# Copying the second key stack on GpSimd, and placing the scores ahead of the second turned half

## The chip, the cores and the metric

One core of a Trainium2 chip runs the whole kernel in one launch. The metric is the device time in microseconds; the median of three runs of the kernel before is 1804.26 us (1802.96 to 1804.39).

## What is computed

A transformer layer on x of 4 batches, 1024 tokens, 256 features, in float32: a layer norm, DeBERTa-style attention with 16 heads of 16 features, a residual, then a layer norm and a feed-forward with 8 experts, picked per token, and a residual again. The change lies in the attention:

```python
scores = einsum('bhqd,bhkd->bhqk', q, k) / scale
c2p = take_along_axis(einsum('bhqd,hpd->bhqp', q, pos_k), c2p_pos, -1)     # by distance, 128 buckets
p2c = swapaxes(take_along_axis(einsum('bhkd,hpd->bhkp', k, pos_k), p2c_pos, -1), -1, -2)
probs = softmax(scores + (c2p + p2c) / scale)
ctx = einsum('bhqk,bhkd->bhqd', probs, v)
```

The bucket depends on the distance q - k alone, and beyond 128 tokens it is constant on either side. So only the three 128x128 blocks around the diagonal need the gathered values (the kernel calls them near), and for all others two constants per row do.

## The kernel before

The program has four stages: `project` (up to about 135 us of the profiled execution), `attend` (to about 1350 us), `mix` and `experts`. The change is in `attend` (L570). There are N = 64 units, one for each batch and head, and each has QT = 8 steps, one for each block of 128 queries; s counts steps over all units, t is the step in a unit, x counts tables. Every engine runs its own loop over s and waits on semaphores, so its order is what the Python text says.

**TensorE** (loop at L822) does in step s, in this order: the first half of a turned block, `flip(back, 0)`, for the block back = s - 13; the position table of block x = s + 20 (`make_table`, two matmuls at L743 and L745 into the one bank `table_ps`); the second turned half `flip(back, 1)`; the scores `score(s)` of block s; in every second step `weigh` for two blocks (sums of probabilities times values, L810); and once per unit, at t = 1, `turn_top` (L818). A flip makes 512 columns of transposed scores in one of two PSUM banks `flip_ps` (L789 for far blocks, L796 for near ones). It waits for `expd`, the exponential that read the same bank one block earlier. `make_table` waits for `table_kept` of the table before, and at t = 2 also for `top_kept`, since the turned row maxima use the same bank. `score(s)` (far blocks L766, near blocks L773) waits for `seen` of block s - 2, at t = 0 for `twin_made` and the loads, and ahead of L773 for `near_made`. With j for the block of `back` within its unit, j = (t + 3) mod 8.

**ScalarE** (loop at L954) does in step s: `exponent(back, 0)` (L932), `keep_table` (L924 and L925, the table from PSUM into `table`), `exponent(back, 1)`; at t = 4 the `twin` of the next unit (L938: the key stack `after`, 96 partitions x 1024 bfloat16, is copied into `before`, the second key stack, whose other rows differ); at the end of a unit's flips `keep_sum`; and at t = 1 `keep_top`: a copy (L944) and a DMA issue (L946) that puts the row maxima into `quest`, where `flip` of j = 0 needs them (`top_in`, L782).

**VectorE** (L906) does in step s `look(s)`: the maximum of the far scores (L849), then `level(s - 1)` (L870), then near scores plus near table with the row maximum (L859, this signals `seen`); and once per unit `normalise` (L878 to L885; L882 is its multiplication).

**GpSimd** (L1040) makes the near part of a unit out of what DMAs bring: five steps `edge` (L995, L998, L1003, L1008, L1011) for each of two parts h = 0 (three blocks) and h = 1 (five blocks), placed by the list `steps` (L1033); each part ends in one count of `near_made`. It also does `keep_side` (L983) and, at t = 7, `split_top` (L1021 to L1031), which waits for `seen` of the whole unit and feeds `turn_top`.

**SP** (L703) is a queue of DMA issues, in order, with waits between them. For each u: `skew_write(u+2, 0)` puts half of a unit's tables into DRAM with a pitch that skews them, `skew_read(u+1, 1)` reads the skewed near part h = 1 back, `load_unit(u+4)` loads queries and keys (four DMAs, L178; it waits until the flips of the unit that used the buffers are done), every second time `load_far`, `skew_write(u+2, 1)`, `skew_read(u+2, 0)`, `store(u-3)`. A `skew_read` waits for the landing of its `skew_write` (L690). Ahead of the loop stands `load_unit(2)`.

Of the kernel before, what the change touches and what calls it, by code (L numbers as in the profile page):

```python
# [21 lines left out]
N = B * H  # L22
QT = S // P
# [18 lines left out]
KROWS = TERMS * DH  # L42
# [5 lines left out]
BUFS = 6  # L48
HATS = 4
# [520 lines left out]
def attend(nc, sem, spent, masks, rows, hats, split_d, far_d, v_d, skew_d, ctx_d):  # L570
# [13 lines left out]
    with ExitStack() as ctx:  # L584
# [43 lines left out]
        def live(s):  # L628

            return 0 <= s < TS  # L630
# [31 lines left out]
        def _(sp):  # L662
# [36 lines left out]
                sp.dma_start(view(ctx_d, n * (P * 2 * P), [[2 * P, P], [1, 2 * P]]), made[n % 2][:, :]  # L699
                             ).then_inc(ctx_out[n % 2], 16)  # L700

            load_unit(EARLY)
            for u in range(-2, N + 3):  # L703
                if 0 <= u + 2 < N:
                    skew_write(u + 2, 0)
                if 0 <= u + 1 < N:
                    skew_read(u + 1, 1)
                if EARLY < u + 4 < N:
                    load_unit(u + 4)
                if EARLY <= u + 2 < N and u % FARS == 0:  # L710
                    load_far(u + 2)
                if 0 <= u + 2 < N:
                    skew_write(u + 2, 1)
                    skew_read(u + 2, 0)
                if 0 <= u - 3 < N:
                    store(u - 3)
                if u == 1:
                    for semaphore in spent:
                        sp.sem_clear(semaphore)
                if u % BATCH == 4 and u // BATCH + 1 < B:  # L720
                    load_vals(u // BATCH + 1)
# [4 lines left out]
        def _(pe):  # L726
# [95 lines left out]
            for s in range(-AHEAD, TS + LAG + 1):  # L822
                back = s - LAG
                if live(back):
                    flip(back, 0)
                if live(s + AHEAD):
                    make_table(s + AHEAD)
                if live(back):
                    flip(back, 1)
                if live(s):  # L830
                    score(s)
                if live(back - 1) and back % 2 == 0:
                    weigh(back - 2)
                    weigh(back - 1)
                if s > QT and s % QT == 1 and s // QT <= N:
                    turn_top(s // QT - 1)
# [78 lines left out]
        def _(act):  # L915
# [16 lines left out]
                nc.scalar.activation(probsT[s % 4][:, half * 512:(half + 1) * 512], flip_ps[half][:, :], ACT.Exp,  # L932
                                     scale=SCALE).then_inc(expd, 1)

            def twin(n):
                i = n % BUFS
                act.wait_ge(hats_in[i], 16 * HATS * (n // BUFS + 1))
                nc.scalar.copy(before[i][0:KROWS, :], after[i][0:KROWS, :]).then_inc(twin_made, 1)  # L938

            def keep_top(n):  # L940
                act.wait_ge(top_turned, n + 1)
                if n >= 2:
# [11 lines left out]
            for s in range(-AHEAD, TS + LAG + 1):  # L954
                if s == 6 - AHEAD:
                    act.wait_ge(set_up, 4)
                    act.wait_ge(before_set, 3)
                    for dst, src in ((quests[KROWS:FAR, :, :], ones[0:3, :]), (afters[FAR:ROWS, :, :], after_rows[:, :]),
                                     (befores[FAR:ROWS, :, :], before_rows[:, :])):
                        nc.scalar.dma_start(dst, src.unsqueeze(1).to_broadcast([dst.shape[0], BUFS, S])).then_inc(rows_set, 16)  # L960
                if s == 10 - AHEAD:
                    hats.load_vals(nc.scalar, v_d, 0)
                back = s - LAG
                if live(back):
# [2 lines left out]
                    keep_table(s + AHEAD)  # L967
                if live(back):
                    exponent(back, 1)
                if s % QT == 4 and 0 <= s // QT + 1 < N:  # L970
                    twin(s // QT + 1)
                if live(back - 1) and (back - 1) % QT == QT - 1:
                    keep_sum((back - 1) // QT)
                if s > QT and s % QT == 1 and s // QT <= N:
# [3 lines left out]
        def _(pool):  # L978
            def keep_side(n, h):
                wait_tables(pool, n * QT + 4 * h + 3)  # L980
                if n >= 3:
                    pool.wait_ge(edge_made, (n - 3) * 10 + 10)
                nc.gpsimd.tensor_copy(side[n % 3][:, :, 4 * h:4 * h + 4], table[n % 2][:, h, :, :, BAND]).then_inc(side_kept, 1)  # L983

            def edge(n, h, step):
                i = n % 2
# [53 lines left out]
            for s in range(-AHEAD, TS):  # L1040
# [5 lines left out]
                for at, h, of in steps:  # L1046
                    n = (s - at) // QT + 1
                    if (s - at) % QT == 0 and 0 <= n < N:
                        for step in of:
                            edge(n, h, step)  # L1050
                if live(s) and t == QT - 1:
                    split_top(u)

# [697 lines left out]
```

## Time and profile before

| | us |
|---|---|
| median of three runs | 1804.26 |
| the profiled execution, its time | 1804.36 |
| its span in the profile | 1802.5 |
| PE busy in the span | 1630.6 (90%) |
| DVE busy | 1350.3 (75%) |
| ACT busy | 1135.2 (63%) |
| POOL busy | 1035.2 (57%) |

PE is TensorE, PEld its weight loads, DVE VectorE, ACT ScalarE, POOL GpSimd, SP the queue of SyncE. The spans of matmuls overlap, since they are pipelined, and their ends are modelled; the distance from start to start tells more than the durations. The busy shares are means over four stages; the middle of the attention, where unit follows unit in the same pattern, is what the rows below show.

### The profile page before, as it was taken

Reading aid. Unit: us, or ns where it says so; the run is one execution under the profiler, and the core shown is the slowest. Engines: PE = TensorE matmul, PEld = TensorE weight load, DVE = VectorE, ACT = ScalarE, POOL = GpSimd, SP = SyncE. Lnnn points to the kernel's source line nnn. Section 1 sums busy time; section 2 is a strip of 40 time slices with the busy share of each in tenths; the row PEclk is TensorE's granted clock in tenths of the full one; section 3 lists DMA queues with packets and bytes.
Section 4 is the critical chain, followed back from the end, with each engine's and each line's share of the span. In section 5 each row is a group of like instructions: output and inputs, shape, how many; then the busy total and the mean of one; then the engine's idle time right before and its main releaser. Section 6 shows DMA issues by size and latency. Waiting matters only on the chain. (4 is left out here: it accounts for less than half of the span.)

```text
span 1802.5 us, 41947 instructions
## 1 busy us (share of the span) xinstructions
PE 1630.6 (90%) x13688; PEld 1149.4 (64%) x13688; DVE 1350.3 (75%) x3868; ACT 1135.2 (63%) x2764; POOL 1035.2 (57%) x1264
## 2 busy tenths in 40 slices
PE   7964899999999999999999999999986856999997
PEld 4532566666666666666666666666643646999996
DVE  4754888888888888888888888888956854555553
ACT  6852677777777777777777777777753731222221
POOL 0004776777777777777777777777714622333332
PEclk9985999999999999999999999999996957999998
DMA  4977888788787878788878787777608625666661
GB/s 138 331 279 249 265 284 261 257 265 273 261 282 262 282 253 276 243 278 275 274 252 272 258 277 252 264 266 263 229 13 206 207 71 183 204 191 197 206 197 63
DMA packets 292451, 421.67 MB, mean 234 GB/s; under 512 B 35382, under 2 KB 233804, under 8 KB 292139
## 3 DMA queue, kind: packets, MB, share of 16 engines
q1 hardware_dynamic: 271640, 378.99, 64.3%
q10 hardware_dynamic: 16851, 30.67, 5.5%
q0 software_dynamic: 3744, 9.31, 1.4%
q8 instruction: 112, 1.84, 0.4%
q14 instruction: 104, 0.85, 0.1%
HBM read 241.39 MB, written 177.79 MB: 233 GB/s over the span
## 5 line engine op out<-in xcount | busy, mean ns | idle before, releaser
L932 ACT ACTIVATE t_probsT<-t_flip 128x512 f32<-128x512 f32 x1024 | 612.8, 623 | 204.2 <-PE t_flip L796 122.3
L849 DVE TENSOR_REDUCE t_most<-t_scores 128x1 f32<-128x640 f32 (+1 forms) x512 | 436.1, 852 | 157.8 <-PE t_scores L773 157.2
L859 DVE CUSTOM_DVE_ANT_0 t_band<-t_scores,t_near,t_most 128x384 f32<-128x384 f32 (+1 forms) x512 | 297.3, 581 | 0.5 <-DVE t_most L849 0.2
L870 DVE TENSOR_SCALAR_CACHE_REDUCE t_band<-t_band,t_top 128x384 f32<-128x384 f32 (+1 forms) x512 | 291.2, 569 | 0.0
L924 ACT COPY t_table<-t_table_ps 128x388 f32<-128x388 f32 x502 | 248.5, 495 | 48.1 <-PE t_table_ps L745 45.0
L810 PE MATMUL t_sum_ps<-t_probsT,vals 128*32 128x256 f32 x4096 | 274.3, 385 | 0.3 <-ACT t_probsT L932 0.3
L1011 POOL TENSOR_TENSOR t_near<-t_near,masks 128x768 f32<-128x768 f32 (+1 forms) x128 | 268.4, 2097 | 0.0
L796 PE MATMUL t_flip<-masks,t_band 128*128 128x128 f32 x1408 | 260.0, 273 | 0.0
L773 PE MATMUL t_scores<-masks,t_near 128*128 128x128 f32 x1408 | 241.9, 275 | 14.8 <-POOLq L1014 14.7
L766 PE MATMUL t_scores<-afters,quests 105*128 105x256 bf16 (+3 forms) x1024 | 244.0, 288 | 1.2 <-DVE t_top L859 1.2
L995 POOL TENSOR_TENSOR t_near<-t_near,masks 128x384 f32<-128x384 f32 (+1 forms) x128 | 146.2, 1142 | 168.6 <-DMA t_near<-skew_d 164.3
L773 PEld LDWEIGHTS t_scores<-masks,t_near 128*128 128x128 f32 x1408 | 181.8, 143 | 54.0 <-POOLq L1014 16.6
L766 PE MATMUL t_scores<-befores,quests 105*128 105x256 bf16 (+3 forms) x768 | 193.2, 292 | 0.0
L789 PE MATMUL t_flip<-quests,afters 108*128 108x512 bf16 (+3 forms) x512 | 159.4, 311 | 11.9 <-ACT t_probsT L932 10.2
L789 PE MATMUL t_flip<-quests,befores 108*128 108x512 bf16 (+3 forms) x512 | 159.2, 313 | 9.1 <-ACT t_probsT L932 4.1
L796 PEld LDWEIGHTS t_flip<-masks,t_band 128*128 128x128 f32 x1408 | 163.0, 141 | 3.3
L743 PE MATMUL t_table_ps<-rows,quests 96*128 96x194 bf16 x502 | 126.6, 252 | 42.4 <-ACT t_table L925 18.2
L810 PEld LDWEIGHTS t_sum_ps<-t_probsT,vals 128*32 128x32 f32 x4096 | 106.8, 109 | 87.4 <-issue 41.2
L1717 PEld LDWEIGHTS e_hid_ps<-e_xT,e_w 128*128 128x128 f32 x1248 | 147.3, 194 | 5.2 <-ACT e_xT L1583 3.2
L1717 PE MATMUL e_hid_ps<-e_xT,e_w 128*128 128x128 f32 x1248 | 147.9, 277 | 2.6 <-ACT e_xT L1583 2.6
L925 ACT COPY t_table<-t_table_ps 128x124 f32<-128x124 f32 x502 | 146.7, 292 | 0.0
L1008 POOL TENSOR_TENSOR t_near<-t_near,masks 128x384 f32<-128x384 f32 (+1 forms) x128 | 146.4, 1144 | 0.0
(212 smaller groups left out, 2546.2 us busy)
## 6 DMA issues: line engine op xcount, KB each, us to landing
skew_d<-t_table SPq DMA_DIRECT2D x128, 1024.0 KB, 9.6
t_near<-skew_d SPq DMA_DIRECT2D x128, 640.0 KB, 8.0
t_near<-skew_d SPq DMA_DIRECT2D x128, 384.0 KB, 7.5
e_w<-in_L_ffn_W_dram ACTq DMA_DIRECT2D x39, 512.0 KB
e_w<-in_L_ffn_W_dram SPq DMA_DIRECT2D x39, 512.0 KB
split_d<-p_part SPq DMA_DIRECT2D x32, 384.0 KB, 3.3
afters<-split_d SPq DMA_DIRECT2D x128, 96.0 KB
quests<-split_d SPq DMA_DIRECT2D x128, 96.0 KB
```

What stands on the lines that cost most here:

```text
L766: nc.tensor.matmul(out[:, at:at + size], quest[i][0:XROWS, t * P:(t + 1) * P], keys[0:XROWS, piece[0] * P:piece[0] * P + size], start=at % ...
L773: last = nc.tensor.matmul(out[:, (j - lo) * P:(j - lo + 1) * P], near[n % 2][:, 1, j, (t - j + 1) * P:(t - j + 2) * P], ident, start=False ...
L789: last = nc.tensor.matmul(out[:, (a - lo) * P:(z - lo) * P], keys[:, j * P:(j + 1) * P], quest[i][:, a * P:z * P], start=first, stop=False ...
L796: last = nc.tensor.matmul(out[:, (t - lo) * P:(t - lo + 1) * P], band[n % 2][:, t, at:at + P], ident, start=False, stop=True, is_transpose ...
L810: last = nc.tensor.matmul(sum_ps[32 * g:32 * g + 32, 0:2 * P], vals[b % 2][:, j, h * VDIM:h * VDIM + 32], probsT[s % 4][:, g * 2 * P:(g + ...
L849: nc.vector.tensor_reduce(most[:, c:c + 1], out[:, wide:S], AX.X, ALU.max).then_inc(far_seen, 1)
L859: nc.vector.tensor_tensor_reduce(band[n % 2][:, t, 0:wide], out[:, 0:wide], near[n % 2][:, 0, t, at:at + wide], 1.0, most[:, c:c + 1], ALU ...
L870: nc.vector.tensor_scalar(band[n % 2][:, t, 0:wide], band[n % 2][:, t, 0:wide], top[n % 2][:, t:t + 1], None, ALU.subtract, ALU.max, accum ...
L924: nc.scalar.copy(ends, table_ps[:, :, 0:FEW].rearrange("p a (e v) -> p a e v", e=2))
L932: nc.scalar.activation(probsT[s % 4][:, half * 512:(half + 1) * 512], flip_ps[half][:, :], ACT.Exp, scale=SCALE).then_inc(expd, 1)
L1011: nc.gpsimd.tensor_tensor(tail, tail, masks[:, 1, :].unsqueeze(1).unsqueeze(1).to_broadcast([P, 2, many, P]), ALU.mult).then_inc(edge_made, 1)
L1717: last = nc.tensor.matmul(hid_ps[s % 2][:, c, :], w1[s % WB][:, f, c * P:(c + 1) * P], xT[s % 2][:, f, :], start=(f == 0), stop=(f == 1))
```

## The change

- GpSimd makes the second key stack: `twin` moves from ScalarE's loop (t = 4) to GpSimd's (t = 2, after the `edge` step of that slot).
- On TensorE `score(s)` stands ahead of `flip(back, 1)`; before it stood behind it.
- On the SP queue `load_unit(2)` and `skew_read(0, 0)` swap sides: the read of the first near part comes right behind `skew_write(0, 0)`, and `load_unit(2)` behind the read. Only then comes `skew_write(0, 1)`.
- ScalarE issues the first load of the values at s = 0 and no longer at s = -10.

```diff
--- before.py
+++ after.py
@@ -699,18 +699,20 @@
                 sp.dma_start(view(ctx_d, n * (P * 2 * P), [[2 * P, P], [1, 2 * P]]), made[n % 2][:, :]
                              ).then_inc(ctx_out[n % 2], 16)
 
-            load_unit(EARLY)
             for u in range(-2, N + 3):
                 if 0 <= u + 2 < N:
                     skew_write(u + 2, 0)
                 if 0 <= u + 1 < N:
                     skew_read(u + 1, 1)
-                if EARLY < u + 4 < N:
+                if u == -2:
+                    skew_read(0, 0)
+                if EARLY <= u + 4 < N:
                     load_unit(u + 4)
                 if EARLY <= u + 2 < N and u % FARS == 0:
                     load_far(u + 2)
                 if 0 <= u + 2 < N:
                     skew_write(u + 2, 1)
+                if 1 <= u + 2 < N:
                     skew_read(u + 2, 0)
                 if 0 <= u - 3 < N:
                     store(u - 3)
@@ -825,10 +827,10 @@
                     flip(back, 0)
                 if live(s + AHEAD):
                     make_table(s + AHEAD)
+                if live(s):
+                    score(s)
                 if live(back):
                     flip(back, 1)
-                if live(s):
-                    score(s)
                 if live(back - 1) and back % 2 == 0:
                     weigh(back - 2)
                     weigh(back - 1)
@@ -932,11 +934,6 @@
                 nc.scalar.activation(probsT[s % 4][:, half * 512:(half + 1) * 512], flip_ps[half][:, :], ACT.Exp,
                                      scale=SCALE).then_inc(expd, 1)
 
-            def twin(n):
-                i = n % BUFS
-                act.wait_ge(hats_in[i], 16 * HATS * (n // BUFS + 1))
-                nc.scalar.copy(before[i][0:KROWS, :], after[i][0:KROWS, :]).then_inc(twin_made, 1)
-
             def keep_top(n):
                 act.wait_ge(top_turned, n + 1)
                 if n >= 2:
@@ -958,7 +955,7 @@
                     for dst, src in ((quests[KROWS:FAR, :, :], ones[0:3, :]), (afters[FAR:ROWS, :, :], after_rows[:, :]),
                                      (befores[FAR:ROWS, :, :], before_rows[:, :])):
                         nc.scalar.dma_start(dst, src.unsqueeze(1).to_broadcast([dst.shape[0], BUFS, S])).then_inc(rows_set, 16)
-                if s == 10 - AHEAD:
+                if s == 0:
                     hats.load_vals(nc.scalar, v_d, 0)
                 back = s - LAG
                 if live(back):
@@ -967,8 +964,6 @@
                     keep_table(s + AHEAD)
                 if live(back):
                     exponent(back, 1)
-                if s % QT == 4 and 0 <= s // QT + 1 < N:
-                    twin(s // QT + 1)
                 if live(back - 1) and (back - 1) % QT == QT - 1:
                     keep_sum((back - 1) // QT)
                 if s > QT and s % QT == 1 and s // QT <= N:
@@ -981,6 +976,11 @@
                 if n >= 3:
                     pool.wait_ge(edge_made, (n - 3) * 10 + 10)
                 nc.gpsimd.tensor_copy(side[n % 3][:, :, 4 * h:4 * h + 4], table[n % 2][:, h, :, :, BAND]).then_inc(side_kept, 1)
+
+            def twin(n):
+                i = n % BUFS
+                pool.wait_ge(hats_in[i], 16 * HATS * (n // BUFS + 1))
+                nc.gpsimd.tensor_copy(before[i][0:KROWS, :], after[i][0:KROWS, :]).then_inc(twin_made, 1)
 
             def edge(n, h, step):
                 i = n % 2
@@ -1048,6 +1048,8 @@
                     if (s - at) % QT == 0 and 0 <= n < N:
                         for step in of:
                             edge(n, h, step)
+                if t == 2 and 0 <= u + 1 < N:
+                    twin(u + 1)
                 if live(s) and t == QT - 1:
                     split_top(u)
```

## Rows read from the trace of the kernel before

**Rows 1.** Busy time by engine, 300 to 1250 us: PE, PEld, DVE, ACT, POOL; clock; DMA share; GB/s
```profile
300.00:1250.00 950.00, 916.13 (x8824) 609.38 (x8823) 825.99 (x2295) 737.68 (x1828) 707.64 (x889) 1.00 0.80 266
```

**Rows 2.** Waits, 300 to 1250 us: total us, times, longest; SPq is the queue
```profile
PEld t_flip L789 <- ACT t_probsT L932: 61.5, 222, 0.4
...
DVE t_most L849 <- PE t_scores L773: 118.5, 210, 0.8
...
POOL t_near L995 <- DMA t_near<-skew_d: 116.6, 87, 4.1
...
POOL t_top_part L1021 <- DVE t_top L859: 107.0, 42, 3.9
...
PEld t_flip L789 <- DMA quests<-t_topT: 0.5, 1, 0.5
...
SPq L178 <- PE t_flip L796: 229.8, 52, 6.1
```

**Rows 3.** Timeline of PE over one unit, 690 to 709 us: start us, duration us
```profile
692.46 0.25 PE L743 MATMUL t_table_ps<-rows,quests 96*128 96x194 bf16 x1
...
692.81 0.39 PE L789 MATMUL t_flip<-quests,afters 108*128 108x512 bf16 x1
...
696.52 0.26 PE L743 MATMUL t_table_ps<-rows,quests 96*128 96x194 bf16 x1
...
697.02 0.28 PE L789 MATMUL t_flip<-quests,afters 108*128 108x256 bf16 x1 [0.16 <-ACT t_probsT L932]
...
699.79 0.24 PE L743 MATMUL t_table_ps<-rows,quests 96*128 96x194 bf16 x1
...
701.79 0.24 PE L743 MATMUL t_table_ps<-rows,quests 96*128 96x194 bf16 x1 [0.24 <-ACT t_table L925]
...
702.20 0.23 PE L789 MATMUL t_flip<-quests,befores 108*128 108x128 bf16 x1
...
704.69 0.25 PE L743 MATMUL t_table_ps<-rows,quests 96*128 96x194 bf16 x1
...
704.87 0.27 PE L789 MATMUL t_flip<-quests,befores 108*128 108x256 bf16 x1
...
706.30 0.25 PE L743 MATMUL t_table_ps<-rows,quests 96*128 96x194 bf16 x1
...
706.59 0.39 PE L789 MATMUL t_flip<-quests,afters 108*128 108x512 bf16 x1
```

**Rows 4.** Timeline of ACT in the same unit, 699 to 702 us
```profile
699.39 0.26 ACT L944 CAST t_topT<-t_table_ps 24x128 bf16<-24x128 f32 x1 [0.89 <-PE t_table_ps L818]
...
699.68 0.73 ACTq L946 DMA_DIRECT2D quests<-t_topT  x1
...
700.51 0.60 ACT L932 ACTIVATE t_probsT<-t_flip 128x512 f32<-128x512 f32 x1 [0.86 <-PE t_flip L796]
...
701.00 0.48 ACT L924 COPY t_table<-t_table_ps 128x388 f32<-128x388 f32 x1
```

**Rows 5.** Groups by shape: busy us, mean ns of one, idle before
```profile
L938 ACT COPY befores<-afters 96x1024 bf16<-96x1024 bf16 x52 | 54.7, 1053 | 0.0
...
L995 POOL TENSOR_TENSOR t_near<-t_near,masks 128x512 f32<-128x512 f32 x52 | 66.6, 1281 | 67.2 <-DMA t_near<-skew_d 67.2
...
L1035 POOL MEMSET t_before_rows<- 9x1024 bf16 x1 | 0.9, 942 | 134.9 <-POOLq L223 134.9
```

**Rows 6.** Two lines of VectorE, whole run: duration in ns, min/median/max
```profile
L859 DVE CUSTOM_DVE_ANT_0 t_band<-t_scores,t_near,t_most x512: 478/612/619, 168.0 to 1327.0; 128x384 f32<-128x384 f32 x128, 128x256 f32<-128x256 f32 x43
...
L882 DVE TENSOR_TENSOR t_turned<-t_turned,t_share x64: 291/292/984, 222.3 to 1348.7; 128x128 f32<-128x128 f32 x64
```

**Rows 7.** Timeline of the SP queue at the start of attention
```profile
141.59 4.48 SPq L683 DMA_DIRECT2D skew_d<-t_table  x2
...
148.74 1.97 SPq L693 DMA_DIRECT2D t_near<-skew_d  x2
...
154.64 1.24 SPq L693 DMA_DIRECT2D t_near<-skew_d  x2
```

## Prediction of the time after the change

> **What bounds the kernel now.** I read the busy time of the engines over the middle of the attention first, then the waits there, then one unit on TensorE, then the same unit on ScalarE. From 300 to 1250 us TensorE shows work in 916 of 950 us at a granted clock of 1.00, its upper level of 2.4 GHz; VectorE is next with 826, ScalarE has 738 and GpSimd 708 [rows 1]. 52 units pass in that stretch, one in some 18.2 us. So TensorE sets the pace, and what counts is the time in which it stands. The busy time hides that, because the modelled ends overlap; the waits show it: weight loads of the flips waited 61.5 us for ScalarE's exponential [rows 2], 1.18 us per unit, some of it beside matmuls still running.
>
> The exact size comes from start-to-start distances. A table takes two matmuls, and the second turned half follows it. Where nothing is waited for, the table at 704.69 is followed by the flip at 704.87, so 0.18 us is the clean distance. In four other steps of the unit it is 0.35 (692.46 to 692.81), 0.50 (696.52 to 697.02), 0.41 (701.79 to 702.20) and 0.29 us (706.30 to 706.59) [rows 3]. The excess is 0.17 + 0.32 + 0.23 + 0.11 = 0.83 us per unit. In all of them the second flip waits until ScalarE has read its bank one block earlier: ScalarE takes exponential, table copy, exponential, and TensorE comes to the second flip only 0.18 us behind the table.
>
> A second kind of standing is seen at 699.79 to 701.79: from one table to the next 2.00 us. The chain there is on ScalarE: the copy of the row maxima at 699.39, which the table at 699.79 needs since it uses the same bank; the DMA issue at 699.68, 0.73 us long, in which ScalarE does nothing else; the exponential at 700.51; the table copy at 701.00, for which the next table, at 701.79, waits [rows 3, 4].
>
> **The scores ahead of the second flip.** Between table and second flip now stand the 5 to 7 matmuls of the scores, which need nothing of ScalarE. The two matmuls of a table take 0.18 us from start to start [rows 3], for 194 columns each; those of the scores are 1024 columns in all and two or three near blocks, so at least five times as much work per step: estimate 0.6 us or more. The largest excess is 0.32, so all four go: -0.83 us per unit. What the first flip of the next step waits for, the first exponential, is issued on ScalarE ahead of the second one, and the second exponential now starts up to 0.8 us later in its step. Its price is a burst: exponential, exponential, table copy, 0.5 us each by the starts of rows 4, thus some 2.0 us behind the second flip until the table copy is through and the next table may start. TensorE has two halves, a table, scores and, since every second step ends in `weigh`, always one `weigh` of 1 us in between: about 3 us. No new wait by that reckoning. The 2.00 us block of the row maxima stays: the turned maxima, the copy, the DMA issue, the exponential and the table copy keep their order, and the second flip has no part in it. So TensorE's unit becomes 18.2 - 0.83.
>
> With tables, flips and scores all alive there are steps s = 13 to 491, 479 steps, 60 units. 60 x 0.83 = 50 us. In the last 20 steps with scores there are no tables: perhaps 1 us more in all.
>
> **What must keep up.** VectorE waits 118.5 us / 52 = 2.3 us per unit for scores [rows 2]; 0.83 less leaves 1.4. The scores come earlier in each step, all by about the same, so its rhythm is kept. SP waits 229.8 / 52 = 4.4 us per unit in front of `load_unit` for flips [rows 2]. These second flips now end a step, so `load_unit`, `skew_write(u+2, 1)` and `skew_read(u+2, 0)`, queued behind that wait, start up to 0.8 us later in the step; but the unit is shorter, and the near part read there is used more than a unit later. The share of the DMA engines rises from 0.80 to 0.80 x 18.2/17.35 = 0.84: no bound, though landings may take longer. Here is one that matters: the row maxima are issued at 699.68 and the first flip of j = 0 stands about 6.3 us behind. It waited for that landing once in 52 units, for 0.5 us [rows 2], so landings reach 6.3 to 6.8 us now and then. One of the removed excesses (0.23) lies in between, so about 6.05 us are left. I put 0.05 us per unit on this wait, 3 us in all.
>
> **The copy on GpSimd.** ScalarE loses 1.053 us per unit [rows 5]. It has 950 - 738 = 212 us of idle time, 4.1 per unit, so the removal alone is worth nothing in the old order; in the new one the twin, 1 us in front of an exponential, would have eaten part of the gain at one step. No row shows a one-input GpSimd instruction of 1024 bfloat16. The nearest are a memset of 1024 bfloat16, 0.942 us, as the lower end (it reads nothing), and a two-input one of 512 float32, 1.281 us [rows 5], twice which is 2.6 us, as the upper end. I take 1.1 us, near the memset, for the same count and type. On the path to the end it is hidden by GpSimd's waits for the near part and for the row maxima, (116.6 + 107.0) / 52 = 4.3 us per unit [rows 2]. After the shorter unit and the copy 2.4 us are left (0.9 at the upper end). Behind the copy in GpSimd's order stand the rest of part h = 0 and all of h = 1, and TensorE waits for them by `near_made`; both had room, since GpSimd itself waited for a landing at the head of either part. `twin_made` is needed six steps later.
>
> A rule speaks against putting more on GpSimd. First the rows: the one VectorE instruction here that reads two operands of SBUF, L882, takes 0.292 us in the median and 0.984 at most, so it sometimes stands for about one GpSimd instruction; L859, with one operand in PSUM, never exceeds 0.619 against 0.612, although GpSimd is busy three quarters of the time [rows 1, 6]. The Trainium skill, "SBUF — State Buffer", section "SBUF: two separate sides", says that the two engines share a port pair as an exclusive lock, held for a whole instruction, against VectorE instructions in a two-port mode or with two SBUF inputs. The trace agrees on L882. By the rule alone the sum would not move while L882 is the only one struck, once per unit; were L859 struck too, it is the rival below.
>
> **The start.** `skew_read(0, 0)` waited for `skew_write(0, 0)`, issued at 141.59, until 148.74 [rows 7], and it still does. It lands earlier, without `skew_write(0, 1)` and the values beside it. But `skew_write(0, 1)`, whose issue ended at 141.59 + 4.48 = 146.07, now comes behind the read (1 us) and `load_unit(2)` (3 us), at about 152, 6.5 us later, and `skew_read(0, 1)` was issued upon its landing, 154.64 [rows 7]: some 9 us behind. Step t = 3 needs that part. So the first three scores gain up to 5 us, and all that follows loses up to 6.5, less what the quieter queue gives back: bounds -4 and +6, I take +1.
>
> **Sum.** Against the profiled execution of 1804.4 us: -50 - 1 + 3 + 1 = -47, 1757 us. The median of the runs is 1804.3, so the sum holds for it.
>
> **Rivals.**
> A: as above, with 0.65 to 0.95 us per unit and the start between its bounds: 1741 to 1771. Chance 0.62.
> B: a new wait takes part of the gain. The nearest are VectorE's `seen` (1.4 us of room per unit, but uneven steps), the landing of the row maxima, and `near_made` of h = 1 behind the copy. With half of the gain left, 0.2 to 0.6 us per unit: 60 x 0.4 = 24, 1780 us (1768 to 1792). For it: three margins of 0.1 to 1.5 us in one unit. Chance 0.20.
> C: more goes than I count. If the earlier, evener flow also removes the wait at 701.79 (0.4 us by its 0.24 idle and the load before it): 0.83 + 0.4 = 1.23, x 60 = 74, 1804.4 - 74 + 3 = 1733. Against: that chain is untouched. Chance 0.06.
> D: the port lock. Were L859 held for the copy and GpSimd's other work, up to 1.1 us per unit more on VectorE, which has 1.4: mostly hidden, 0 to 0.5 us, 1757 to 1787. Against: 0.619 at most. Chance 0.03, within the range.
> E: no change. The second flip was never the limit and TensorE waits elsewhere for the same time, VectorE or the near part: 1804 within 3.6. Against: VectorE waits for TensorE. Chance 0.04.
> F: slower. The landing of the row maxima, with the DMA engines at 0.84, waits in front of the flip of j = 0. It decides from a mean of 6.05 + 0.83 = 6.9 us on; each 0.1 us beyond costs 6 us; at 7.2 us the time is 1804 + 18 = 1822. Against: one wait in 52 so far. Chance 0.05.
> That the change does not do what it says can hardly be: the orders are written out.
>
> **How the numbers follow.** The likeliest is A, 1757. A alone gives 1741 to 1771; the range takes in D and the better part of B: 1740 to 1784. About 0.2% or 3.6 us is what a measurement can tell from no change. Faster 0.62 + 0.06 + 0.03 + 0.19 = 0.90, same 0.05, slower 0.05.
>
> **What would show it.** In the changed profile: table to scores 0.18 us in every step, second flips without a wait for the exponential, the two tables around the row maxima still 2.00 us apart, a unit of 17.3 to 17.5 us, VectorE's wait for scores down to about 1.5 us per unit; the copy on GpSimd 0.9 to 1.3 us; first near scores at about 161 us, those of t = 3 later than before. I am wrong if the unit stays above 17.8, or if the flips of j = 0 wait for the row maxima in most units.

## The result, and the profile after

The changed kernel takes 1788.58 us in the median of five runs (1785.86 to 1800.09), the kernel before 1804.26 (1801.67 to 1804.61): ratio 0.993, 95% interval 0.9901 to 0.9959. It is faster by some 16 us; forecast were 47. The profiled execution took 1785.86 us, 18.5 less than that of before.

The page's span and busy times of the changed kernel:

```profile
span 1784.1 us, 41887 instructions
...
PE 1601.9 (90%) x13688; PEld 1149.7 (64%) x13688; DVE 1359.6 (76%) x3868; ACT 1107.0 (62%) x2700; POOL 1093.5 (61%) x1328
```

The middle of the attention by engine, as in [rows 1] (PE, PEld, DVE, ACT, POOL; clock; DMA share; GB/s):

```profile
300.00:1250.00 950.00, 915.25 (x9009) 624.30 (x9007) 855.04 (x2350) 731.38 (x1814) 768.45 (x962) 1.00 0.82 272
```

Busy TensorE time is as before, VectorE's rose from 826 to 855 us and GpSimd's from 708 to 768, because more units pass in the stretch and GpSimd has one instruction more in each. The last two columns went from 0.80 and 266 GB/s to 0.82 and 272: a unit moves the same bytes in less time.

TensorE's timeline in one unit, the places of [rows 3]:

```profile
702.60 0.25 PE L745 MATMUL t_table_ps<-rows,quests 96*128 96x194 bf16 x1
...
702.77 0.60 PE L768 MATMUL t_scores<-afters,quests 105*128 105x256 bf16 x3
...
706.47 0.26 PE L745 MATMUL t_table_ps<-rows,quests 96*128 96x194 bf16 x1
...
706.66 0.27 PE L768 MATMUL t_scores<-afters,quests 105*128 105x256 bf16 x1
...
709.42 0.24 PE L745 MATMUL t_table_ps<-rows,quests 96*128 96x194 bf16 x1
...
711.41 0.24 PE L745 MATMUL t_table_ps<-rows,quests 96*128 96x194 bf16 x1 [0.24 <-ACT t_table L927]
...
711.58 0.27 PE L768 MATMUL t_scores<-afters,quests 105*128 105x256 bf16 x1
...
715.86 0.25 PE L745 MATMUL t_table_ps<-rows,quests 96*128 96x194 bf16 x1
...
716.03 0.27 PE L768 MATMUL t_scores<-afters,quests 105*128 105x256 bf16 x1
```

From table to scores it is 0.17 to 0.19 us in this unit, and in all but 8 of the 426 steps from 300 to 1250 us. The waits of the second turned half, 0.83 us per unit, are gone. The two tables around the row maxima, at 709.42 and 711.41, are still 1.99 us apart.

The unit's length is read from the copy of the sums, which comes once per unit. First the kernel before, then the changed one (the two times are those of the first and the last start):

```profile
L952 ACT COPY t_made<-t_sum_ps x64: 372/411/415, 216.4 to 1347.6; 128x256 f32<-128x256 f32 x64
```

```profile
L949 ACT COPY t_made<-t_sum_ps x64: 372/372/373, 222.7 to 1329.6; 128x256 f32<-128x256 f32 x64
```

From the first to the last sum it was 1131.2 us and is 1106.9, 24.3 less. The first sum comes 6.3 us later, and behind the last one nothing changes (454.9 and 454.5 us to the end of the span). So 24.3 - 6.3 = 18 us, what the profiled executions differ by. From start to start of that copy the units last 18.21 us in the mean before and 17.82 after (units 4 to 55), while forecast were about 17.4. Yet 11 of these 52 last under 17.35 us, the shortest 17.27, and before none in that stretch was below 18.16. So TensorE can run the forecast unit; something else lets it do so only now and then.

The waits from 300 to 1250 us, beside [rows 2], now in 53 units:

```profile
POOL t_near L995 <- DMA t_near<-skew_d: 159.6, 104, 3.7
...
DVE t_most L851 <- PE t_scores L775: 87.2, 133, 2.7
...
PEld t_flip L791 <- ACT t_probsT L934: 76.6, 204, 0.4
...
PEld t_table_ps L820 <- POOL t_top_part L1031: 16.8, 19, 3.1
...
PEld t_scores L775 <- POOLq L1014: 13.6, 32, 0.7
...
PE t_table_ps L820 <- POOL t_top_part L1031: 8.5, 9, 2.6
...
POOL t_top_part L1021 <- DVE t_top L861: 5.1, 4, 2.1
...
PE t_scores L775 <- POOLq L1014: 4.9, 17, 0.4
...
PEld t_flip L791 <- DMA quests<-t_topT: 3.2, 7, 0.8
...
SPq L690 <- DMA skew_d<-t_table: 252.0, 53, 7.2
...
SPq L178 <- PE t_flip L798: 152.7, 51, 5.7
```

TensorE waits newly for `split_top` (L820; before 1.6 us in its weight loads) and for `near_made` (L775), both GpSimd's. The wait of the flips' weight loads for the exponential did not fall (76.6 us, before 61.5), but it moved: before, 58 us of it stood ahead of the second half; now none does, and 66 us stand behind `weigh`, whose matmuls are still running then. GpSimd hardly ever waits for VectorE now (5.1 us, before 107.0); it waits for the landing of the near part (159.6, before 116.6), and by far the most at the head of h = 0 (125.6, before 49.3; at the head of h = 1 34.0, before 67.2). SP waits 252.0 us for landings of `skew_write`, 4.8 per unit (186.8 before), and less for flips (152.7, before 229.8). The list of DMA issues gives 11.1 us in the median from the issue of a `skew_write` to its landing; before it was 9.6.

The start, SP's queue beside [rows 7] and the first near scores on TensorE:

```profile
149.39 1.31 SPq L693 DMA_DIRECT2D t_near<-skew_d  x2
...
150.74 1.49 SPq L178 DMA_DIRECT2D afters<-split_d  x2
...
153.97 1.20 SPq L683 DMA_DIRECT2D skew_d<-t_table  x2
...
163.37 0.93 SPq L693 DMA_DIRECT2D t_near<-skew_d  x2
```

```profile
164.40 0.64 PE L775 MATMUL t_scores<-masks,t_near 128*128 128x128 f32 x2
...
181.29 0.90 PE L775 MATMUL t_scores<-masks,t_near 128*128 128x128 f32 x3 [11.98 <-POOLq L1014]
```

`skew_write(0, 1)` goes out at 153.97, behind the read and the loads of unit 2; before it went out at 145.53 (the second of the two issues that the first of [rows 7] has in one line). Its landing lets `skew_read(0, 1)` go at 163.37, before at 154.64. The first near scores come at 164.40 (166.15 before), but t = 3 has to stand 12 us, until 181.29 (174.42 before).

### The profile page after: what moved, and what is told of

Read it like the earlier page. It is cut to its first block and busy times, and to the rows that moved or that the text cites. A ratio compares the mean times of both kernels' runs of the same rounds, so it can differ in the third digit from the quotient of the medians.

```text
span 1784.1 us, 41887 instructions
## 1 busy us (share of the span) xinstructions
PE 1601.9 (90%) x13688; PEld 1149.7 (64%) x13688; DVE 1359.6 (76%) x3868; ACT 1107.0 (62%) x2700; POOL 1093.5 (61%) x1328
## 5 line engine op out<-in xcount | busy, mean ns | idle before, releaser
L934 ACT ACTIVATE t_probsT<-t_flip 128x512 f32<-128x512 f32 x1024 | 590.7, 605 | 198.7 <-PE t_flip L791 102.9
L861 DVE CUSTOM_DVE_ANT_0 t_band<-t_scores,t_near,t_most 128x384 f32<-128x384 f32 (+1 forms) x512 | 297.0, 580 | 0.4 <-DVE t_most L851 0.2
L775 PE MATMUL t_scores<-masks,t_near 128*128 128x128 f32 x1408 | 243.8, 277 | 18.0 <-POOLq L1014 17.7
L775 PEld LDWEIGHTS t_scores<-masks,t_near 128*128 128x128 f32 x1408 | 179.6, 142 | 66.6 <-POOLq L1014 29.0
## 6 DMA issues: line engine op xcount, KB each, us to landing
skew_d<-t_table SPq DMA_DIRECT2D x128, 1024.0 KB, 11.1
```

The lines of the kernel that those rows point to most:

```text
L775: last = nc.tensor.matmul(out[:, (j - lo) * P:(j - lo + 1) * P], near[n % 2][:, 1, j, (t - j + 1) * P:(t - j + 2) * P], ident, start=False ...
L861: nc.vector.tensor_tensor_reduce(band[n % 2][:, t, 0:wide], out[:, 0:wide], near[n % 2][:, 0, t, at:at + wide], 1.0, most[:, c:c + 1], ALU ...
```

## The experiments

In all, the times are medians, and ratios are to the kernel before in runs on the same chip. "First sum" and "unit" (mean of units 4 to 55, start to start of the copy of the sums) are of the one profiled execution of each; where a kernel was taken twice, the unit differs by 0.04 and 0.08 us.

| kernel | ratio (95%) | median us | first sum | unit |
|---|---|---|---|---|
| before | 1 | 1804.3 | 216.4 | 18.21 |
| after | 0.993 (0.990 to 0.996) | 1788.6 | 222.7 | 17.82 |
| e1, copy back on ScalarE | 0.991 (0.989 to 0.994) | 1789.9 | 223.9 | 17.91 |
| e2, old start | 0.990 (0.987 to 0.992) | 1785.7 | 217.2 | 17.95 |
| e3, copy one slot earlier | 0.993 (0.989 to 0.997) | 1785.0 | 223.8 | 17.79 |
| e4, write and read ahead of the loads | 0.994 (0.991 to 0.997) | 1796.8 | 220.6 | 18.08 |
| e5, before with the scores first | 0.986 (0.984 to 0.989) | 1782.6 | 217.2 | 17.84 |
| e6, before with the copy on GpSimd | 1.000 (0.999 to 1.002) | 1804.5 | 216.6 | 18.21 |
| e7, after, half the bytes written | 0.980 (0.978 to 0.983) | 1768.0 | 220.7 | 17.52 |
| e8, before, half the bytes written | 1.000 (0.999 to 1.002) | 1805.1 | 214.3 | 18.25 |
| e9, write alone ahead of the loads | 0.988 (0.984 to 0.991) | 1783.9 | 223.9 | 17.88 |
| e10, values in eight pieces, old start | 0.990 (0.987 to 0.993) | 1790.0 | 216.7 | 17.99 |
| e11, e10 with e3 | 0.989 (0.987 to 0.991) | 1786.8 | 216.0 | 17.98 |
| e12, e5 with the pieces | 0.987 (0.983 to 0.991) | 1786.9 | 216.2 | 18.00 |
| e13, after, 256 KB more per unit | 1.015 (1.013 to 1.017) | 1833.6 | 221.3 | 18.72 |
| e14, before, 256 KB more per unit | 1.015 (1.014 to 1.017) | 1832.7 | 217.2 | 18.72 |
| e15, after again | 0.990 (0.985 to 0.994) | 1787.3 | 222.3 | 17.90 |
| e16, e5 again | 0.986 (0.984 to 0.988) | 1781.1 | 214.1 | 17.88 |

My first theory (G) was that the copy costs, because it stands in GpSimd's chain from one landing to `near_made`.

**e1: the copy back on ScalarE.**

```diff
-                if t == 2 and 0 <= u + 1 < N:
-                    twin(u + 1)
...
+                if s % QT == 4 and 0 <= s // QT + 1 < N:
+                    twin(s // QT + 1)
```

> The changed kernel with the copy of the second key stack back on ScalarE (t = 4); scores first and the new start stay. Theory G (the copy costs because it stands in GpSimd's chain from the landing of the near part h = 0 to near_made of h = 1): the mean unit falls from 17.8 to about 17.4 us, the wait of PE L820 for split_top nearly goes, time about 1765 us (1758 to 1772). Rival D (the DMA landings alone are late, whoever copies): unit stays at 17.7 to 17.9, time 1784 to 1795. Rival L (the port lock between VectorE and GpSimd): unit falls as in G, but the durations of VectorE's instructions fall too.

Unit 17.91, 1789.9 us: theory G fell. It came out where the rival D, the landings, had put it. GpSimd lost a microsecond of work per unit and only waited longer for landings, 220.2 us for 159.6. The same microsecond does not matter on ScalarE either.

**e3: the copy on GpSimd, one slot earlier.**

```diff
                     if (s - at) % QT == 0 and 0 <= n < N:
+                        if at == 1:
+                            twin(n)
                         for step in of:
                             edge(n, h, step)
-                if t == 2 and 0 <= u + 1 < N:
-                    twin(u + 1)
```

> The changed kernel with the copy still on GpSimd but one slot earlier: at t = 1, behind the last edge step of h = 1 and ahead of the first of h = 0, where GpSimd stands 2 to 3 us for the landing of h = 0. Theory G: the copy costs nothing there, since the landing hides it; mean unit about 17.4, GpSimd's idle time ahead of the 128x384 form of L995 falls from 2.4 to about 1.4 us, time about 1765 us. Rival D: nothing moves, 1784 to 1795. A theory in which GpSimd's busy time as such is the bound also gives no change.

Ratio 0.993, as the change itself; its mean unit of 17.79 is within what repeats differ by (17.82 and 17.90). GpSimd's waits for landings fell to 131.3 us and the time did not.

**e6: the copy on GpSimd in the kernel before**, nothing else.

> The kernel before with the copy of the key stack on GpSimd alone (t = 2), nothing else changed. My prediction says worth nothing: 1804 within 3. A theory in which GpSimd's chain is loaded by it to the point of delay gives over 1808; one in which ScalarE's freed microsecond matters gives under 1797.

1804.5 us, ratio 1.000. Its middle stretch, to be held against [rows 1]:

```profile
300.00:1250.00 950.00, 916.16 (x8826) 609.31 (x8823) 825.62 (x2300) 700.48 (x1776) 758.94 (x941) 1.00 0.80 266
```

ScalarE's time fell by 37 us and GpSimd's rose by 51, all of it hidden. In the old order the copy is worth nothing, as the prediction had it.

**e2: the old start** (`load_unit(2)` ahead of the loop, the read behind `skew_write(0, 1)`, the values at s = -10).

```diff
+            load_unit(EARLY)
             for u in range(-2, N + 3):
...
-                if u == -2:
-                    skew_read(0, 0)
...
-                if s == 0:
+                if s == 10 - AHEAD:
                     hats.load_vals(nc.scalar, v_d, 0)
```

> The changed kernel with the old start: load_unit(2) ahead of the loop, skew_read(0, 0) behind skew_write(0, 1), values loaded at s = -10. If the start costs what the first sum shows (222.7 us after, 216.4 before), the first sum comes at about 216.5 and the time falls by 6 us, to about 1782. If the later units take the lost time back anyway, or if the start's loss is compensated in the first units, no change.

The first sum comes at 217.2 us, 5.5 earlier; the median is 2.9 us lower, where 6 were expected, with overlapping runs. Over all profiles the start is told apart without exception: with the new one the first sum comes at 220.6 to 223.9, with the old one at 214.1 to 217.2.

**e5: the scores first, in the kernel before.**

```diff
+                if live(s):
+                    score(s)
                 if live(back):
                     flip(back, 1)
-                if live(s):
-                    score(s)
```

> The kernel before with the scores ahead of the second turned half and nothing else: the copy on ScalarE, the old start. If the whole gain of the change comes from this one swap, the units are 17.9 us in the mean (as with the copy on ScalarE, e1), the first sum comes at 216.5, and the time is 1782 to 1788. If the copy on GpSimd carries part of the gain, over 1790.

This swap of two calls alone has the whole gain of the units (17.84), and a ratio of 0.986.

**e4 and e9: the order on SP.** e9 puts `skew_write(u+2, 1)` ahead of `load_unit(u+4)`, e4 the read of h = 0 too.

```diff
+                if 1 <= u and u + 2 < N:
+                    skew_write(u + 2, 1)
                 if EARLY <= u + 4 < N:
                     load_unit(u + 4)
...
-                if 0 <= u + 2 < N:
+                if u < 1:
                     skew_write(u + 2, 1)
```

> The changed kernel with skew_write(u+2, 1) and skew_read(u+2, 0) ahead of load_unit(u+4) on the SP queue from u = 1 on, so that they no longer wait for the flips of two units ago and for four load issues (about 3 us). Theory G with its head at the landing of h = 0: the near part lands 2 to 4 us earlier, GpSimd's idle time ahead of L995 128x384 goes to about 0, the near part is no longer late, mean unit 17.3 to 17.4, time about 1762 to 1768. If the DMA engines are the bound and not the order on SP, no change (1784 to 1795), or worse where the loads of the units become late.

> The changed kernel with skew_write(u+2, 1) alone ahead of load_unit(u+4) on the SP queue, from u = 1; skew_read(u+2, 0) stays behind the loads. The write is issued some 5 us earlier against the step, the loads at most 0.6 us later. Theory O or D (late landing of part h = 1): skew_read(u+2, 1), which waited 4.8 us per unit for that landing, goes out earlier, GpSimd no longer waits ahead of L995 128x512, mean unit 17.3 to 17.5 save for the units with a load of values, time 1765 to 1775. If the head of the chain is h = 0 alone, no change (1784 to 1792).

e9 has a unit of 17.88 and 1783.9 us, where both O and D, as put for this run, asked for 1765 to 1775: both missed, and the time is that of the third case, a chain that hangs on h = 0 (1784 to 1792). SP no longer waits for landings of `skew_write` from 300 to 1250 us, yet the reads of part h = 1, issued earlier, now take 10.0 us to land instead of 7.3 (mean of their landings in that stretch): what the order gains, later landings take back. e4 is the slowest of this group; there TensorE's tables stand up to 1.8 us at a time for a releaser that the profile does not name, and by the code the loads of the unit are what is left. Nor did the waits for landings go: none is left at the head of h = 0, and 151.9 us stand at the head of h = 1. Both speak against the order as the cause. That e9's median is 4 us lower than the change's, with runs from 1777 to 1788, says little.

**e7 and e8: half of the bytes of every `skew_write`**, after and before.

```diff
+                many = 4 if n < 2 else 2
...
-                sp.dma_start(view(skew_d, ..., [[PITCH, P], [TABLE, 2], [1, 4 * SPOT]]),
-                             table[n % 2][:, h, :, :, :].rearrange("p a u v -> p a (u v)")) ...
+                sp.dma_start(view(skew_d, ..., [[PITCH, P], [TABLE, 2], [1, many * SPOT]]),
+                             table[n % 2][:, h, :, 0:many, :].rearrange("p a u v -> p a (u v)")) ...
```

> The changed kernel with half of the bytes of every skew_write from unit 2 on (two of the four tables of each half are written, 512 KB for 1024 KB; the others read back what older units left, so the near part of two thirds of the blocks is not theirs). Theory D (the landings of the skewed near part are late since the DMA queues are fuller, whoever copies the key stack): landings of skew_write fall by 3 us or more, GpSimd is ready in time, the mean unit falls from 17.8 to 17.3 or 17.4 us, time 1760 to 1768. Rival O (the bound is the order of waits on the SP queue, in which the write stands behind the flips and the load issues, whatever its bytes): the landing falls too, and with it the unit, but only in part: 17.5 to 17.7, 1770 to 1782. Rival V (VectorE's uneven steps make the late unit): no change, 17.8.

> The same halving in the kernel before. All theories in which the kernel before is bound by TensorE's waits for ScalarE (second flip 0.18 us behind the table): the unit stays at 18.17 us and the time at 1800 to 1805, only the few long units (18.4 to 18.8) go. If it falls by over 10 us, the landings bounded the kernel before too and my reading of it was wrong.

e7's middle stretch and its waits, then e8's stretch:

```profile
300.00:1250.00 950.00, 920.07 (x9161) 634.03 (x9158) 854.84 (x2385) 746.62 (x1844) 786.72 (x976) 1.00 0.73 216
```

```profile
POOL t_top_part L1022 <- DVE t_top L862: 113.4, 54, 3.1
...
POOL t_near L996 <- DMA t_near<-skew_d: 20.7, 36, 2.7
...
PEld t_flip L792 <- DMA quests<-t_topT: 14.1, 22, 1.4
```

```profile
300.00:1250.00 950.00, 913.87 (x8804) 607.34 (x8806) 822.55 (x2291) 736.65 (x1823) 704.35 (x886) 1.00 0.70 207
```

This pair shows what holds which kernel. With 216 GB/s for 272, landings of `skew_write` come after 7.9 us in the median for 11.1, GpSimd's wait for landings falls from 159.6 to 20.7 us, it waits for VectorE again (113.4), and the unit is 17.52 us (median 17.31). The time is 1768.0 us, the upper end of what D asked, but the unit is O's (17.5 to 17.7), so this run alone does not part the two. It is 11 us above the forecast of the change; its first sum comes 4.3 us later than before, where +1 was forecast. So the bytes of the writes account for 0.30 us of the 0.5 by which the unit exceeded the shortest ones, and 0.2 stay with a fifth fewer bytes. Some of that may be the landing of the row maxima: 14.1 us in the waits, 0.26 per unit, for 3.2 in the changed kernel. In the kernel before the same saving gives nothing, ratio 1.000: there TensorE's own order was the bound. The few long units, which were expected to go, stayed (mean 18.25).

**e10, e11, e12: the later loads of values in eight pieces**, one per unit, for one of 1152 KB.

```diff
-                hats.load_vals(sp, v_d, b)
+                sp.dma_start(vals[b % 2][:, k:k + 1, :], view(v_d, (b * QT + k) * (P * VROW), [[VROW, P], [P * VROW, 1], [1, VROW]])
+                             ).then_inc(vals_in[b % 2], 16)
...
-                if u % BATCH == 4 and u // BATCH + 1 < B:
-                    load_vals(u // BATCH + 1)
+                if 4 <= u % BATCH < 4 + QT and 0 < u and u // BATCH + 1 < B:
+                    load_vals(u // BATCH + 1, u % BATCH - 4)
```

> The changed kernel with the old start and with each later load of values (1152 KB at once, in the 5th unit of a batch) cut into eight of 144 KB, one per unit. The three units behind such a load last 20 to 22.5 us in all changed kernels, 3 to 5 us over the others, against 0.5 us in the kernel before. If the burst delays the near part, these units fall to 17.9, the neighbours hardly rise (144 KB are under 3% of a unit's traffic), and the time falls by 8 to 10 us against the old start alone (1785.7), to about 1776. If only the volume counts, no change.

> As the run with the loads of values cut in eight and the old start, and with the copy on GpSimd at t = 1 between the two parts, where it stands for a landing. In e3 the units without a load of values had a median of 17.44 us against 17.50 to 17.63. Expected about 4 us below e10, 1770 to 1776; if e3's lower median was chance, the same as e10.

> The kernel before with the scores first and the loads of values cut in eight, copy on ScalarE, old start. By the landings as the bound the copy's place does not matter, so this equals e10 within 4 us, about 1778. If the copy on GpSimd is worth something once the burst is gone (ScalarE's microsecond ahead of an exponential, 0.4 us by my reckoning of one step), it is 5 to 20 us slower than e10.

The long units did go: the three behind such a load lasted 21.1, 22.5 and 20.3 us in e2 (19.0, 20.6 and 21.2 in the change itself), and in e10 the same three are 18.2, 17.9 and 17.9. But the median of the units rose from 17.63 to 17.90 and the mean did not fall (17.95 and 17.99): my forecast of 1776 was wrong, and so was that of 1770 to 1776 for e11. The groups of eight units that carry the pieces average 18.15 us in e10, and the same units of e2, with the whole load in one of them, 18.20: spreading the bytes gained nothing there. e12, with the copy on ScalarE, is within 4 us of e10 and equal to e11: no difference for the copy's place here.

**e13 and e14: 256 KB more per unit**, after and before: each store of a result issued three times, two of them into a spare tensor.

```diff
+                for k in range(3):
+                    sp.dma_start(view((ctx_d, spare_d, spare_d)[k], ...), made[n % 2][:, :]).then_inc(ctx_out[n % 2], 16)
...
```

> The changed kernel with every store of a unit's result issued three times, two of them into a spare tensor: 256 KB more per unit, 5 to 6% of its traffic. If the amount of DMA traffic per unit is the bound, the unit rises by about 5% of 17.8, 0.9 us, and the time by 40 to 55 us, to 1830 or more, above that of the kernel before. If only the order and the waits count, the added issues cost SP 1.5 us, which its waits hide: within 10 us of 1788.

> The same in the kernel before. Its traffic alone would then ask for about 17.8 + 0.9 = 18.7 us, so if the amount is the bound, the unit rises by about 0.5 us from 18.2 and the time by 20 to 35 us, less than in the changed kernel, and both end up alike. If the kernel before has real room (TensorE's waits for ScalarE bound it, with the DMA engines at 0.80), it stays within 6 us of 1804.

After, then before, each with its middle stretch and three waits:

```profile
300.00:1250.00 950.00, 885.63 (x8608) 598.80 (x8609) 819.46 (x2244) 698.34 (x1734) 732.96 (x918) 0.99 0.83 273
```

```profile
POOL t_near L997 <- DMA t_near<-skew_d: 203.5, 102, 4.3
...
PEld t_table_ps L822 <- POOL t_top_part L1033: 57.0, 48, 4.2
...
PE t_table_ps L822 <- POOL t_top_part L1033: 34.2, 41, 3.7
```

```profile
300.00:1250.00 950.00, 901.58 (x8602) 595.61 (x8602) 816.93 (x2239) 717.95 (x1779) 681.98 (x866) 1.00 0.83 273
```

```profile
POOL t_near L997 <- DMA t_near<-skew_d: 253.1, 102, 5.0
...
PEld t_table_ps L820 <- POOL t_top_part L1033: 38.1, 47, 3.4
...
PE t_table_ps L820 <- POOL t_top_part L1033: 16.7, 22, 2.9
```

Both have a unit of 18.72 us and both take some 1833 us, as expected if the traffic binds. The change has lost all its gain, and both move 273 GB/s over this stretch, one more than the changed kernel. The kernel before rose by 28 us on 5% more bytes. An estimate of its room: 5% of 18.2 is 0.9 to 1.0 us and it rose by 0.5, so it had some 0.5 us per unit. Not only the bytes grew, though: the added stores hold SP for some 1.3 to 1.5 us each as they are issued, 3 us per unit and not the 1.5 expected, and all behind them goes out later. SP still stands waiting for 6.2 and 5.0 us per unit, and e9 had shown its order to cost little, but no run adds the issues without the bytes.

**e15 and e16: the change, and the scores first alone, side by side.**

> The changed kernel once more, beside the next. Ratio to before 0.990 to 0.994 as at first.

> The kernel before with only the scores first, once more. By the first sums its start is worth 5 to 6 us against the changed kernel and the copy's place nothing: 3 to 8 us faster than the changed kernel on the same chip. If both are alike, the earlier ratio of 0.986 was that chip's.

1787.3 and 1781.1 us, 6.3 us apart, as much as the start costs; ratios 0.990 and 0.986. The intervals overlap, but e5 and e1, which differ by the start alone, show the same (0.986 and 0.991). The other two pairs are less clear: the change and e2, which also differ by the start alone, have 0.993 and 0.990, and e2 and e5, which differ by the copy's place alone, 0.990 and 0.986, all with touching or overlapping intervals. So the best version that computes the whole result is the kernel before with its scores placed first: faster than before by 1.4%, twice measured, and than the full change by some 6 us in the runs side by side, which is likely and not certain.

## Why the prediction was wrong

**The scores first: right.** Table to scores is 0.17 to 0.19 us, the 0.83 us are gone, the block of 2.00 us stayed at 1.99, and the shortest units, 17.27 to 17.31, are about what 18.17 - 0.83 = 17.34 gives. The term of 50 us is this saving times 60 units, and it supposes that every unit can be as short; the mean unit is 17.82, just above the 17.8 that the prediction had named as the sign of being wrong.

**What must keep up: the step that failed.** The prediction put it so: "The share of the DMA engines rises from 0.80 to 0.80 x 18.2/17.35 = 0.84: no bound, though landings may take longer." Together with the sentence that both parts of `near_made` "had room, since GpSimd itself waited for a landing at the head of either part", that is what failed: the landings held the kernel. With half of the bytes of `skew_write` gone, the changed kernel's unit falls from 17.82 to 17.52 us and its time from 1788.6 to 1768.0 (e7), while the kernel before gains nothing (e8); with 5% more bytes the gain is lost (e13). A wait at the head of GpSimd's chain is no room. It says that `near_made` comes when the landing comes, and with the copy taken off GpSimd the wait grew by as much and the time stayed (e1). The row that could have warned stood in [rows 2]: GpSimd's 116.6 us of waits for landings, which I counted as cover for the copy.

Why the landings came too late: the unit before moved 18.21 us x 266 GB/s = 4.84 MB, the shorter unit has to move the same, and the landing of a `skew_write` went from 9.6 to 11.1 us in the median. How much was lost cannot be worked out from a highest rate. At 273 GB/s, where e13 and e14 end up, 4.84 MB take 17.7 us, close to the 17.82 measured, but 273 is a mean and no ceiling: the changed kernel itself moves 278 GB/s from 381.7 to 555.9 us and 286 from 503.4 to 555.9, the kernel before 314 from 545.0 to 563.4, in a unit of 18.5 us with a load of values in it (share 0.92), and at 216 GB/s e7 is still 0.2 us over its shortest units. So some 0.3 of the 0.5 us goes with the bytes of the writes; the rest is open. A candidate is the landing of the row maxima, which the prediction put at 0.05 us per unit and which is 0.26 in e7. What in the traffic makes the landings late (sizes of the pieces, writes against reads, the memory) was not tried.

**The rivals.** B, a new wait takes part of the gain, is what happened, by one of its three places, `near_made` and the row maxima behind it; it gave 1768 to 1792 us. That the time lies in there is partly luck: its size was half by guess, it named `near_made` of h = 1 behind the copy, while the wait grew at the head of h = 0 and the copy had no part in it (e1), and the cause behind it, the bytes, I had not named. F, the landing of the row maxima, cost 3.2 us of waits in all (weight loads, 300 to 1250 us). D, the lock that holds L859, is not seen: that line, now L861, stays at 0.612 us in the median and 0.619 at most. But the instruction with two SBUF operands, now L884, has doubled in the median, against [rows 6]:

```profile
L884 DVE TENSOR_TENSOR t_turned<-t_turned,t_share x64: 291/610/1221, 228.5 to 1330.7; 128x128 f32<-128x128 f32 x64
```

39 of the 64 are over 0.32 us, 7 before, and every one of them ends 0.15 us behind the end of a GpSimd instruction. That agrees with the Trainium skill's rule ("SBUF — State Buffer", section "SBUF: two separate sides"), which speaks of instructions with two SBUF operands or in a two-port mode. The copy is not what does it: with the copy alone added (e6) the unit stays at 18.21 and VectorE's busy time at 826 us, and e5, without it, has 39 long ones too. It is 17 us of VectorE's time in all 64 units, beside 87.2 us of its waits for scores.

**The copy: right in price and worth.** 1.1 us forecast, and the profile has

```profile
L983 POOL COPY befores<-afters x64: 1026/1032/1063, 158.1 to 1285.3; 96x1024 bf16<-96x1024 bf16 x64
```

It is worth nothing in the old order (e6) and nothing in the new (e1, e3). That it would have eaten part of the gain on ScalarE was wrong, or hidden by the landings: e5, with the copy on ScalarE, is the fastest with all bytes. The runs cannot tell these two apart.

**The start: mis-sized.** I took +1 within -4 and +6; it is +6.3, just beyond the end. `skew_write(0, 1)` comes 8.4 us later and not 6.5 (153.97 for 145.53, forecast 152); its 9 us to land were right, and the read behind it is 8.7 us later. Of these 2.4 came back by the first sum. The first near scores, forecast at 161, gained 1.75 us and not 5: the data landed 5.0 us earlier (GpSimd's first step on it is at 155.60 for 160.63), but the scores came at 164.40.

**Sum.** Forecast -50 - 1 + 3 + 1; in the profiled execution it is -24.3 from the first to the last sum, and +6.3. The bounds of A, 1741 to 1771, leave out the 3 us of the row maxima and the 1 us of the last steps; with them they are 1745 to 1773, which changes nothing here.

## What to carry to other kernels

Do not call a transfer queue free because its busy share is under 1, and do not count an engine's wait for a landing as room for what comes after it. Look for the engine that waits for landings at the head of a chain, and ask what happens to that chain when the unit gets shorter and its bytes do not. One run with fewer bytes and one with more, each in the kernel before too, show whether the landings hold the kernel. And where a change has several parts, time them alone: here one swap had the whole gain, the copy's place showed none, and the new start put the first sum 6 us later.

## What the runs showed of the hardware

- This mix of writes and reads (1 MB skewed writes, reads of 384 and 640 KB, some small ones) came to a mean of 272 to 273 GB/s at a DMA share of 0.82 to 0.83 from 300 to 1250 us in the changed kernel, e3, e5, e13 and e14, at a granted clock of 0.99 to 1.00. That is no ceiling: a load of values beside it makes 314 GB/s at 0.92 for one unit (kernel before, 545.0 to 563.4 us), and from 45 to 90 us other transfers show 331 GB/s at 0.99.
- At such a share landings can decide the time: a fifth fewer bytes made the changed kernel 20 us faster (e7).
- The unit behind a load of 1152 KB lasted 1.5 to 3.7 us over the median in the changed kernel and 2.6 to 4.9 in e2; in the kernel before, which had room, 0 to 0.6.
- The median landing of a 1 MB skewed write was 9.6 us at 266 GB/s, 11.1 at 272, but 10.5 and 11.0 at 273 (e13, e14); that of half of it 7.9 at 216. The mean rate alone does not give it.
- A GpSimd copy of 96 x 1024 bfloat16 takes 1.03 us; ScalarE's took 1.05.
- A VectorE multiplication of 128x128 float32 with both operands in SBUF took 0.29 us or, 39 times of 64 in the changed kernel, up to 1.22; each of the 39 ended 0.15 us behind the end of a GpSimd instruction. L861, with one operand in PSUM, was never held so (0.619 at most in 512).
